# Heads of two chunks as one group, with projections, decays and accumulation in later steps

## What is computed

```python
proj = input_states @ in_proj_w.T                 # gate 8192, xBC 8192 + 2*8*128, dt 128
xBC = silu(conv(xBC) + conv_b)                    # 4 taps, causal
dt = softplus(dt + dt_bias);  dA = dt * A         # A = -exp(A_log)
y_intra = einsum('bcijh,bcjhp->bcihp', (C.B) * exp(cum_i - cum_j) * dt, xc)
y = y_intra + y_inter + D * x
g = y * silu(gate)                                # per group of 1024 channels:
g = g * rsqrt(mean(g*g) + EPS) * norm_w
return g @ out_w.T
```

## Time and profile before

| | us |
|---|---|
| median of 3 runs (3007.71 to 3009.3) | 3008.96 |
| the profiled execution | 3009.73 |
| its span, first to last instruction | 3007.9 |
| PE busy | 2905.6 (97%) |
| DVE busy | 2024.6 (67%) |
| ACT busy | 1366.0 (45%) |
| POOL busy | 1251.1 (42%) |
| mean granted PE clock | 0.979 of full |

### The profile page before, as it was taken

One profiled execution on the slowest core, in us unless ns is written; L12 is line 12 of the kernel. 1 busy time (PEld: TensorE's weight loads), 2 busy tenths in 40 slices (PEclk: granted clock), 3 DMA queues, 4 the chain that ended last, 5 costly groups with the idle time before them and its releaser, 6 DMA issues.

```text
span 3007.9 us, 56310 instructions
## 1 busy us (share of the span) xinstructions
PE 2905.6 (97%) x22224; PEld 2292.7 (76%) x22224; DVE 2024.6 (67%) x3144; ACT 1366.0 (45%) x2025; POOL 1251.1 (42%) x820
## 2 busy tenths in 40 slices
PE   3999999999999999999999999999999999999986
PEld 2777777777778777787877778787777877777764
DVE  4787777787666657776666665777566665666656
ACT  2556556555443443443444444344344344444422
POOL 2666666666333433333333333433333343333332
PEclk7999999999999999999999999999999999999985
DMA  5787787778655655655665565655565565565510
GB/s 180 258 269 266 256 270 254 244 261 268 194 173 184 189 179 168 189 184 174 203 188 174 188 189 161 190 181 176 185 197 185 172 191 182 168 194 183 172 36 15
DMA packets 179267, 578.27 MB, mean 192 GB/s; under 512 B 25216, under 2 KB 31872, under 8 KB 170816
## 3 DMA queue, kind: packets, MB, share of 16 engines
q1 hardware_dynamic: 179008, 574.66, 59.8%
HBM read 460.29 MB, written 114.29 MB: 191 GB/s over the span
## 4 chain that ended last, share of the span: by engine, by line
PE 92%; DVE 5%; ACT 1%; issue 1%; DMA 1%; POOL 0%; SPq 0%; ACTq 0%; DVEq 0%; POOLq 0%
PE p_in L431 53%; PE p_out L431 23%; PE p_y L431 10%; PE p_in L510 4%; DVE cv L1125 1%; PE p_y L601 1%; DVE o_ring L1067 1%; ACT w_ring L763 0%; DVE acb L1184 0%; DVE sm L1271 0%; DVE cpar L1108 0%; ACT o_ring L763 0%; DVE sc L1259 0%; DMA decay<-cum_scr 0%; PE p_y L620 0%
## 5 line engine op out<-in xcount | busy, mean ns | idle before, releaser
L431 PE MATMUL p_in<-xnb,w_ring 128*128 128x512 f32 x6912 | 1735.3, 401 | 13.8 <-DVE cv L1125 9.6
L431 PEld LDWEIGHTS p_in<-xnb,w_ring 128*128 128x128 f32 x6912 | 1263.5, 189 | 286.3 <-issue 14.7
L1447 POOL TENSOR_TENSOR g_lo<-g_f,g_hi 128x512 fp32r<-128x512 f32 x256 | 375.6, 1467 | 1248.5 <-ACT g_hi L763 1248.5
L1125 DVE SCALAR_TENSOR_TENSOR cv<-p_in,cpar,cv 128x504 f32<-128x504 f32 (+2 forms) x960 | 703.4, 733 | 118.7 <-ACT cv L763 94.9
L431 PE MATMUL p_out<-o_ring,g_hi 128*128 128x512 f32 x2048 | 648.1, 397 | 0.0
L763 ACT ACTIVATE cv<-p_in,cpar 128x512 f32<-128x512 f32 x320 | 247.9, 777 | 734.3 <-PE p_in L431 689.7
L1160 DVE SCALAR_TENSOR_TENSOR t_y<-x_t,dpar,p_y 128x256 f32<-128x256 f32 x512 | 222.8, 476 | 397.6 <-PE p_y L431 395.2
L431 PEld LDWEIGHTS p_out<-o_ring,g_hi 128*128 128x128 f32 x2048 | 382.4, 188 | 91.1
L763 ACT ACTIVATE sg<-p_in 128x512 f32<-128x512 f32 x256 | 153.5, 600 | 628.3 <-PE p_in L431 628.2
L431 PE MATMUL p_out<-o_ring,g_lo 128*128 128x512 f32 x1024 | 405.4, 396 | 0.0
L1149 DVE TENSOR_TENSOR x_tok<-p_in,dts 128x512 f32<-128x512 f32 x256 | 176.9, 691 | 299.0 <-PE p_in L510 295.5
(11 more groups left out here) (233 smaller groups left out, 2244.3 us busy)
## 6 DMA issues: line engine op xcount, KB each, us to landing
w_ring<-ws_scr SPq DMA_DIRECT2D x432, 512.0 KB, 3.4
o_ring<-ows_scr SPq DMA_DIRECT2D x192, 512.0 KB, 3.4
ws_scr<-w_ring SPq DMA_DIRECT2D x144, 512.0 KB, 4.8
decay<-cum_scr SPq DMA_DIRECT2D x128, 512.0 KB, 6.6
raw_w<-wt SPq DMA_DIRECT2D x144, 256.0 KB, 4.1
ows_scr<-o_ring SPq DMA_DIRECT2D x64, 512.0 KB, 6.2
raw_o<-owt SPq DMA_DIRECT2D x64, 256.5 KB, 5.4
acb<-x SPq DMA_DIRECT2D x3, 1024.0 KB, 7.8
```

The costliest lines, as they stand in the source:

```text
L431: return nc.tensor.matmul(o, lhsT=l, rhs=r, start=first, stop=last)
L1125: ins = V.scalar_tensor_tensor(acc[:, :, t:SEQ], src[:, :, 0:SEQ - t], cpar[:, 5 * m + 3 - t:5 * m + 4 - t], acc[:, :, t:SEQ], ALU.mult, A ...
L1447: T(g_lo[:, c % 2, :], g_f[:, c % 2, :], g_hi[:, c % 2, :].bitcast(F32), ALU.subtract).then_inc(glo_done, 1)
```

## The change

- PE: the heads of chunks c and c+1 (c even) are one group of 64 products, in steps 2, 4 and 6 and, for the last two chunks, in the first step of the next group. The first chunk goes to columns 0 to 255 of the two banks of `p_y`, the second to columns 256 to 511. One wait and one increment (by 2) for both.
- `skipped`, `gated`, `g_high`, `square`, `g_low` and `sum_squares` follow in pairs, in even steps, behind that step's conv. Within ACT's even steps `silu` comes ahead of `gate`. `sg` has three buffers.
- `project(c)` comes in step c + 3 instead of c + 2; `mean_squares` and the first half of `project(7)` after unit 5, the second half in step 2.
- `variance` moves to step 1, `inverse_rms` on POOL to step 2 behind that step's pair of `g_low`, `accumulate` to step 2.
- `decayed(1)` is in step 5 (was 4), `clamped(0)` of the next group in step 7 (was 6), `clamped(1)` in step 1 (was 2). In the very first group `exp(0)`, `differences(0)`, `clamped(0)` and `decayed(0)` come in step 1 and `by_token(0)` after unit 3.
- DVE's `low` and `result` move from late(2) to early(3), `query` to late(3), the moments of an opening tile to early(3); the `softplus` parts are dealt out anew; `by_token` and `tokens_out` of a coming block move from step 1 to step 3.
- One `outs_of` per step; the two splits of o before the loop go. The buffer `xnt` is dropped, tiles are normalized in place in `xt`.

```diff
+GATES = 3
-            return {6: (CPG,), 7: (CPG + 1,)}.get(step, (step + 2,) if 0 <= step < CPG - 2 else ())
+            return (step,) if step >= 0 else ()
@@ SP
-            for c in range(2):
-                split_out(0, c)
-                if tile > QT:
-                    sp.wait_ge(xn_done, tile)
+                sp.wait_ge(xtr_done, tile)
@@ PE, slot and slot_read
-                pe.wait_ge(yread, CPG * n + k)
+                if k == 1:
+                    pe.wait_ge(cbt_done, n + 1)
+                    if not first(n):
+                        pe.wait_ge(msv_done, n)
+                elif k % 2 == 1:
+                    slot_read(k - 1, tb, g)
+                else:
+                    pe.wait_ge(yread, CPG * n + k)
-                if k == 1 and is_at(tb, g, 7):
+                if k == 3 and is_at(tb, g, 7):
                     by_token(tb + 1)
@@ PE, heads
-                pe.wait_ge(xtok_done, CPG * n + c + 1)
-                if c == 0:
-                    if not first(n):
-                        pe.wait_ge(msv_done, n)
-                else:
+                pe.wait_ge(xtok_done, CPG * n + c + 2)
+                if c > 0:
                     pe.wait_ge(yread, CPG * n + c)
-                slot_read(c, tb, g)
+                slot_read(c + 1, tb, g)
+                for cc in (c, c + 1):
+                    for q in range(QT):
+                        col = (cc % 2 * QT + q) * SEQ
...
+                ins.then_inc(y_done, 2)
@@ PE, body
                 if begun:
-                    heads(CPG - 1, *before, n - 1)
+                    heads(CPG - 2, *before, n - 1)
                 unit(1, tb, g, n)
                 if begun:
-                    project(CPG - 2, *back)
-                else:
+                    project(CPG - 3, *back)
+                unit(2, tb, g, n)
+                unit(3, tb, g, n)
+                if not begun:
                     pe.wait_ge(dtr_done, 1)
                     by_token(0)
                 state_products(n)
                 if begun:
-                    project(CPG - 1, *back, range(0, 2))
-                    mean_squares(n - 1)
+                    project(CPG - 2, *back)
                 to_tokens(0, n)
                 unit(4, tb, g, n)
-                heads(0, tb, g, n)
                 unit(5, tb, g, n)
                 if begun:
-                    project(CPG - 1, *back, range(2, QT))
+                    mean_squares(n - 1)
+                    project(CPG - 1, *back, range(0, 2))
                 slot(1, tb, g, n)
...
                     unit(2 + 2 * k, tb, g, n)
-                    heads(k - 1, tb, g, n)
+                    if k % 2 == 0:
+                        heads(k - 2, tb, g, n)
                     unit(3 + 2 * k, tb, g, n)
-                    project(k - 2, tb, n)
+                    if k >= 3:
+                        project(k - 3, tb, n)
+                    elif begun:
+                        project(CPG - 1, *back, range(2, QT))
@@ ACT, body, steps 1 to 7
                     tap0(2 + k, n)
-                    gate(k, n)
-                    silu(2 + k, n)
-                    g_high(k - 1, n)
+                    if k % 2 == 0:
+                        silu(2 + k, n)
+                        gate(k, n)
+                        g_high(k - 2, n)
+                        square(k - 2, n)
+                        square(k - 1, n)
+                        g_high(k - 1, n)
+                    else:
+                        gate(k, n)
+                        silu(2 + k, n)
+                    if k == 1 and not begun:
+                        exp(0, n)
@@ DVE, early
-                if k == 6 and is_at(tb, g, 4):
-                    softplus(tb + 1, (2,))
...
+                if is_at(tb, g, 4) and k == 7:
+                    softplus(tb + 1, (0,))
+                if is_at(tb, g, 5) and k in (1, 3, 7):
+                    softplus(tb + 1, {1: (2,), 3: (3, 4, 5), 7: (6, 7, 8)}[k])
+                if is_at(tb, g, 6) and k in (1, 3, 7):
+                    softplus(tb + 1, {1: (9, 10), 3: (11, 12), 7: (13,)}[k])
@@ DVE, body
-                if begun:
-                    skipped(CPG - 1, n - 1)
                 dve.wait_ge(par_done, n + 1)
                 conv(0, n)
                 if begun:
-                    gated(CPG - 1, n - 1)
+                    skipped(CPG - 2, n - 1)
+                    skipped(CPG - 1, n - 1)
...
                 for k in range(1, CPG):
-                    skipped(k - 1, n)
                     conv(2 + k, n)
-                    gated(k - 1, n)
-                    if k == 2:
-                        clamped(1, n)
-                    if k == 4:
+                    if k % 2 == 0:
+                        skipped(k - 2, n)
+                        skipped(k - 1, n)
+                        gated(k - 2, n)
+                        gated(k - 1, n)
+                    if k == 1 and begun:
+                        variance(n - 1)
+                    if k == 5:
                         decayed(1, n)
-                    if k == 6 and not final(n):
+                    if k == 7 and not final(n):
                         clamped(0, n + 1)
                     early(k, tb, g)
                     x_tokens(k, n)
-                    if k == 1 and begun:
+                    if k == 1:
+                        if not begun:
+                            clamped(0, n)
+                            decayed(0, n)
+                        clamped(1, n)
+                    if k == 2 and begun:
                         accumulate(*back)
@@ POOL, body
-                if begun:
-                    inverse_rms(n - 1)
...
-                    g_low(k - 1, n)
-                    if k >= 2:
+                    if k % 2 == 0:
+                        g_low(k - 2, n)
+                        if k >= 4:
+                            sum_squares(k - 2, n)
                         sum_squares(k - 1, n)
+                        g_low(k - 1, n)
+                    if k == 2 and begun:
+                        inverse_rms(n - 1)
                     if k == 1:
+                        if not begun:
+                            differences(tb, g, 0, n)
                         differences(tb, g, 1, n)
```

More of the change, by code:

```diff
@@ L459, in _ @@
             for q in range(QT):
-                normal_tile(q, (xnt, xt)[q % 2], p_out[q])
+                normal_tile(q, (t_y[:, 0, :], xt)[q % 2], p_out[q])
             pe.wait_ge(wdl_done, 1)
@@ L726, in _ @@
             iterations(pe, body)
[L727 removed]
+            heads(CPG - 2, NTB - 1, GROUPS - 1, ITERS - 1)
+            project(CPG - 3, NTB - 1, ITERS - 1)
             project(CPG - 2, NTB - 1, ITERS - 1)
@@ L886, in body @@
                 tap0(0, n)
+                silu(0, n)
                 tap0(1, n)
-                silu(0, n)
+                silu(1, n)
                 if begun:
+                    g_high(CPG - 2, n - 1)
+                    square(CPG - 2, n - 1)
+                    square(CPG - 1, n - 1)
                     g_high(CPG - 1, n - 1)
-                    square(CPG - 1, n - 1)
-                silu(1, n)
-                if not begun:
-                    tokens_out(0)
-                    exp(0, n)
                 refill(-1)
@@ L1058, in _ @@
                     lows(q - 1)
-                normal(q, (xnt, xt)[q % 2][:, :], acb[:, 0, q, :], q - 1 if q >= 2 else None)
+                normal(q, (t_y[:, 0, :], xt[:, :])[q % 2], acb[:, 0, q, :], q - 1 if q >= 2 else None)
             lows(QT - 1)
@@ L1191, in early @@
                 t, u, tile = opening(tb, g), closing(tb, g), coming(tb, g)
+                y0, y1 = p_y[:, 0, :], p_y[:, 1, :]
                 S = loop_tile
-                if k == 2 and t is not None:
+                if k == 1 and tile is not None:
+                    normal(tile, xt[:, :], xt[:, :], tile)
+                if k == 3 and former(u) is not None:
+                    result(u - 1, S, y0)
+                if k == 3 and tile is not None:
+                    tok = slice((tile % QT) * P, (tile % QT + 1) * P)
+                    low(tile, xnb[(tb + 1) % 2][:, 1, :, tok], xnb[(tb + 1) % 2][:, 0, :, tok], y1)
+                if k == 3 and t is not None:
                     if t == 0:
@@ L1351, in body @@
                 conv(1, n)
-                if not begun:
-                    clamped(0, n)
-                    dve.wait_ge(dtk_done, 2)
-                steps(tb, g)
+                if begun:
+                    gated(CPG - 2, n - 1)
+                    gated(CPG - 1, n - 1)
+                    steps(tb, g)
                 conv(2, n)
                 products(n)
-                dve.wait_ge(cbt_done, n + 1)
-                decayed(0, n)
-                if begun:
-                    variance(n - 1)
+                if not begun:
+                    dve.wait_ge(dtk_done, 2)
+                    steps(tb, g)
+                else:
+                    dve.wait_ge(cbt_done, n + 1)
+                    decayed(0, n)
```

(10 more changed lines are left out.)

85 lines of the change are left out of this document (37 added, 48 removed).

## The result

The changed kernel takes 3103.18 us (median of 4 runs, 3100.56 to 3108.99) beside 3008.34 (3006.03 to 3009.3) of the kernel before on the same chip: ratio 1.0319, 95% interval 1.0301 to 1.0337. It is 95 us slower, where 2991 was forecast.

The account below looks back on a forecast made before the run. TensorE (PE), busy 97% of the span, was taken to bound the kernel. 3009.7 - 45 + 39 + 17 - 17 - 10 - 2 = 2991.7, the median 0.8 lower, so 2991 us; range 2960 to 3018.

Parts of the forecast that it names:

- Term 1: PE's groups of heads: pairing turns 256 into 128, saving 0.35 us of entry and exit each; 45 us saved.
- Term 2: PE before project(0): waits for DVE's accumulate behind POOL's late inverse_rms, at most 2.3 us a group; 39 us lost.
- Term 3: Carried along by that wait: x_tokens(3) late 9 us, tokens_out 6, small ones 2; 17 us lost.
- Term 4: Token block 0: PE's waits for first convolutions and for late x_tokens or low go; 17 us gained.
- Term 5: The start: earlier transposes and decays bring the first pair of heads near 78; 10 us gained.
- Term 6: The tail: one more projection after the last heads fills the wait of mean_squares; 2 us gained.
- What else moves costs nothing: Remaining moves priced at nothing, among them decayed(1) in step 5, ending 5 us before step 6's pair needs it.
- B: Steps 3 and 4: DVE's hold in step 2 costs each group 1 us more; +31, 3022; chance 17%.
- D: Heads: pairing saves nothing, entry and exit paid per chunk or the double group slowed; 3036; chance 4%.
- C: PE loses clock after each of 30 waits, 1.4 us each; +42, 3033; chance 5%.
- the second row: PE's unit after 1.80 us idle took 2.97 us, without clock loss; after 3.20 us idle it took 4.37.

Follow-up runs that it names:

- e10_twice: The kernel before with each of the 32 small products of a chunk's heads issued twice; 3116.73 us, ratio 1.0359.
- e2: The changed kernel with decayed(1) back in step 4 and inverse_rms left late; 3051.48 us, ratio 1.0144.
- e3: The changed kernel with inverse_rms at the head of POOL's step 2 and decayed(1) back in step 4; 2975.19 us, ratio 0.989.
- e1_rms: The changed kernel with inverse_rms back at the head of POOL's step 2; 3019.11 us, ratio 1.004.
- e6_late5: On top of e3, DVE's experts and sums of step 5 come behind x_tokens(5) and scored; 2961.12 us, ratio 0.9841.
- e4_dif6: The changed kernel with POOL's differences for the next group in step 6 instead of step 5; 3052.38 us, ratio 1.0145.

## Why the prediction was wrong, point by point

**Term 1, pairing, -45: right.** 1.44 us a group in kernels without waits, 46 over 32 groups; e10_twice gives the price of the products. One slip in the working did no harm: 13 / 0.184 is 71 per us, and 1/71 is 0.0141, so the earlier trace rows gave 0.45 for 32 products and 47 us saved; that the 0.0146 written in its place is what e10_twice measured is luck.

**Term 2, the wait for acb, +39: right in place, number and size of the waits** (38.4 in 28, none in the groups with step_sizes), too low in what a wait costs, which is the next point.

**Term 3, what it carries along, +17: the waits are about right, what waits cost beyond their length is missing.** e2 less e3 gives terms 2 and 3 together: 76, where 56 stood. To see where the 20 are, take the stretch from the second group's first state product to the last group's, and split it into PE's idle and busy time; the last column is the part of the busy time in which the granted clock was at its lower level, 1.2 GHz.

| | length | idle | busy | at 1.2 GHz |
|---|---|---|---|---|
| before | 2656.9 | 13.7 | 2643.2 | 3.4 |
| after | 2757.9 | 122.3 | 2635.6 | 50.4 |
| e1_rms | 2674.9 | 59.7 | 2615.1 | 26.4 |
| e2_dec4 | 2704.5 | 86.8 | 2617.6 | 17.0 |
| e3_rms_dec4 | 2633.5 | 32.1 | 2601.4 | 3.4 |
| e6_late5 | 2616.4 | 16.6 | 2599.7 | 0.0 |

From e3 to e2 the idle time grows by 55: 40 for acb and 14 for all else, where term 3 had 17 (x_tokens(3) late 4.2 in five places instead of 9 in six; tokens_out 2.3 instead of 6; t_y, sg and xnb the rest). The busy time grows by 16 although the work is the same: about 7 at the lower clock (an estimate, half of the 13.6 us more at 1.2 GHz) and some 9 that the waits cost beyond their listed length, at full clock. One pair of groups shows the latter alone: the last length of e4_dif6 is 1.81 above that of e6_late5 (88.47, 86.66), and its only wait is 1.57 us. The other 5 of the 76 lie before and behind the stretch.

"Near nothing" at the next transposes was right: waits for sg, xnb and x_t in front of transposes grow by 4 us in all.

**Term 4, waits that go in block 0, -17: did not come.** From the second group's first state product to the ninth's it is 611.7 us in the kernel before and 603.0 in e6_late5: 8.7 less, where pairing alone gives 7 x 1.44 = 10. So nothing else was gained; PE's idle time in that stretch is 13.4 us before and 15.1 in e6_late5. The waits for cv did go (0.9 us left of 6.1 between 95 and 700 us); waits for x_t (5.0), sg (4.4) and t_y (3.0) stand in their place. ACT's order is where they arise: skip, a table load of 1.28 us behind it, then x_t and sg.

**Term 5, the start, -10: too large by some 5.** Transposes came at 62.01 (forecast 62), the first pair at 81.13 (forecast 78). The second group began 6.5 us earlier than before, 1.4 of them pairing. The 3 us of the first pair are DVE standing still beside POOL again, in the changed kernel's timeline:

```profile
68.12 7.51 POOL L1520 TENSOR_TENSOR decay<-decay,cumk 128x2048 f32<-128x2048 f32 x2
...
72.61 4.10 DVE L1154 TENSOR_SCALAR decay<-decay 128x2048 f32<-128x2048 f32 x1
```

The clamp takes 1.2 us alone and 4.10 beside POOL's second differences. This one has a single SBUF source; why it stood still is in no run here. The Trainium skill's same section has it that instructions in a mode with two ports contend as well; which mode the clamp ran in, the trace does not show. That alone it takes 1.2 us for 2048 columns, where decayed takes 2.29, would fit.

**Term 6, the tail, -2: right** (about 2 in the changed kernel, from the last group's state products to PE's last matmul, pairing taken off: 185.2 before, 181.5 after).

**"What else moves costs nothing: ... decayed(1) in step 5 ends 5 us before the pair of step 6 needs it": this is the step that failed.** It cost 52 us (44 without the late rms). The margin was counted to the end of `decayed` itself, with the duration that it has in a step where POOL has nothing long. In the first timeline above that even holds: decayed ends at 2687.73, and PE stands before the pair from 2692.23. In the second it ends at 2783.45 and PE is there at 2785.01. The margin of what is queued behind it on DVE, x_tokens(5) and scored, was not counted; nor was the instruction with which POOL meets it there. A second reason was on the list of rivals and priced at nothing in the sum, the lower clock behind waits: it took some 24 of the 95 us (below). The kernel before already had a sign of the first in its trace:

```profile
2681.02 2.29 DVE L1144 TENSOR_TENSOR decay<-decay,cbt 128x2048 f32<-128x2048 f32 x1
2681.84 2.60 POOL L1447 TENSOR_TENSOR g_lo<-g_f,g_hi 128x512 fp32r<-128x512 f32 x1 [2.87 <-ACT g_hi L763]
```

g_lo, 1.30 us alone, has 2.60 where it meets `decayed`, and starts to run when that ends, at 2683.31. At 2.60 it was hidden; moved beside 3.7 us of differences it was not.

**The rivals.** B was right that a second wait would make the kernel slower, and wrong in its place, its cause and its size. It looked for 1 us a group in steps 3 and 4, from DVE's hold in step 2; what came stands in front of the pair of step 6, has another cause and is larger (0.94 and 2.96 us in the two groups of e1_rms against e3_rms_dec4, 3.7 and 4.7 for both causes). D falls by e10_twice.

C, a loss of clock after each of 30 waits, +42 at 5%, is right in good part. Between 100 and 2890 us the granted clock is at its lower level, 1.2 GHz, in 14 stretches of the changed kernel, 51 us in all; in one of the kernel before, 3.4 us; in seven of e1_rms, 27 us; in five of e2_dec4, 17 us. Half of the time that PE was busy in them is 25 us in the changed kernel against 2 in the kernel before (an estimate of what was lost). They follow waits for sc_l (seven of the eleven), for acb (three), for t_y in front of a slot (three) and one "issue". "The waits of term 2 are 2.3 at most, nearer to the second row; I price no clock loss in them" was thus wrong, and two rows were too few to tell: the same length comes with either level. After 1.97 us for acb and after 1.85 in front of a pair the clock fell, and after another 1.85 it did not (in each row the third number from the end is the granted clock):

```profile
823.60:827.00 3.40, 3.40 (x11) 2.69 (x12) 3.29 (x6) 1.34 (x2) 0.00 (x0) 0.68 0.61 228
2418.90:2422.30 3.40, 3.40 (x68) 2.90 (x57) 3.33 (x8) 0.63 (x1) 0.00 (x0) 0.50 0.18 71
2786.90:2790.30 3.40, 3.40 (x74) 2.95 (x75) 3.33 (x7) 0.49 (x1) 0.00 (x0) 1.00 0.18 71
```

The parts of the sum, from the runs: -47 (e6_late5 against before), +14 (experts ahead of x_tokens), +76 (the late rms), +44 (decayed(1)), +8 (the last two together) = +95.

**Left open:** where in the first token block the 3 to 4 us of an earlier start are given back. The waits for sg grow, but what makes silu late there was not isolated. Nor is it known what decides after which wait of some 2 us the clock falls.

## What to carry to other kernels

When an instruction of DVE with two operands in SBUF is moved, look up what GpSimd runs in the new place, and add the longer of the two to everything queued behind either. Count a margin to the last instruction in the queue that PE needs, not to the moved one. Price a lower clock behind every new wait of about 2 us as a possibility, not as nothing. And split a change of many moves into its parts: here the whole without two of its side moves is 33 us faster than the kernel before, and those two, a few lines each, cost 128.

## What the runs showed of the hardware

- A DVE instruction with two SBUF operands and one of POOL's did not run at the same time: whichever came second stood still until the other ended, and the trace writes that as duration: 3.66 us for 16 columns (alone 0.16), 5.74 for POOL's 3.70, 5.02 for 2.29. A median far below the mean of an unchanged line is the sign (`decayed` in after: 2385 ns against 2878).
- Going into and out of the 64x64 products costs 0.36 us a time (1.44 us a group for four fewer, e6_late5 against before); each product 0.0146 (3.73 us for 256, e10_twice).
- A wait of PE costs more than its listed length: 1.81 us for a listed 1.57 at full clock (e4_dif6 against e6_late5, last length), 1.93 for 1.85 in front of a pair (after against e2_dec4, next to last), and 2.88 for 1.37 us more where the clock fell (the same two, last).
- The granted clock fell to 1.2 GHz behind waits of 1.85 to 2.98 us in the changed kernel, and behind others of 1.85 to 2.77 us it stayed at 2.4.
